# A second sort in fewer steps, a bias kept in a freed matrix row, and the combining of moe_1 spread over three attentions

## The reference, cut to what matters

```python
    logits = xt @ Wr + br;  p = softmax(logits);  probs, idx = top_k(p, 2)
    probs = probs / probs.sum(axis=-1, keepdims=True)
    h = jnp.einsum('td,edf->etf', xt, W1) + b1[:, None, :]
    h = _layernorm(jax.nn.relu(h), g1, be1)
    y = jnp.einsum('etf,efd->etd', h, W2) + b2[:, None, :]
    y = _layernorm(jax.nn.relu(y), g2, be2)
    out = jnp.einsum('te,etd->td', gate, y)      # gate: probs at the two chosen experts
```

## Time and profile before

| | |
|---|---|
| PE busy | 1710.9 us (90%) |
| PE weight loads | 1127.0 us (59%) |
| DVE busy | 1166.0 us (61%) |
| ACT busy | 778.5 us (41%) |
| POOL busy | 761.2 us (40%) |
| mean granted clock of the PE | 0.936 |
| transfers | 90.40 MB in 62796 packets |

### The profile page before, as it was taken

One profiled execution on the slowest core, in us unless ns is written; L12 is line 12 of the kernel. 1 busy time (PEld: TensorE's weight loads), 2 busy tenths in 40 slices (PEclk: granted clock), 3 DMA queues, 4 the chain that ended last, 5 costly groups with the idle time before them and its releaser, 6 DMA issues. The chain is left out here.

```text
span 1907.3 us, 30893 instructions
## 1 busy us (share of the span) xinstructions
PE 1710.9 (90%) x10309; PEld 1127.0 (59%) x10309; DVE 1166.0 (61%) x3041; ACT 778.5 (41%) x1965; POOL 761.2 (40%) x983
## 2 busy tenths in 40 slices
PE   5796698768899999999999997879999999999999
PEld 4544476535575657756577564546756565656656
DVE  6836666546756657657576564557757555554654
ACT  2411254315443646537466273126627422232222
POOL 3433545618746636656266462007647200000000
PEclk7865899889999999999999997989999999999999
DMA  8010022100000000000000000000000473643452
GB/s 299 1 28 13 27 81 70 40 17 15 9 1 1 2 1 1 1 1 2 1 2 1 1 2 1 1 1 1 1 1 2 133 204 120 201 120 113 130 168 84
DMA packets 62796, 90.40 MB, mean 47 GB/s; under 512 B 11056, under 2 KB 29104, under 8 KB 61872
## 3 DMA queue, kind: packets, MB, share of 16 engines
q1 hardware_dynamic: 60592, 84.23, 14.4%
q0 software_dynamic: 2048, 4.20, 0.8%
HBM read 78.43 MB, written 9.96 MB: 46 GB/s over the span
## 5 line engine op out<-in xcount | busy, mean ns | idle before, releaser
L1583 POOL TENSOR_TENSOR rows<-rows,rinv 128x512 f32<-128x512 f32 x192 | 197.1, 1054 | 139.6 <-DVE rinv L1821 139.6
L2492 ACT ACTIVATE region_b<-psum 128x512 f32<-128x512 f32 x132 | 78.8, 597 | 259.1 <-PE psum L2454 259.0
L1747 ACT ACTIVATE rows<-psum,nmax 128x512 f32<-128x512 f32 x192 | 130.2, 684 | 125.0 <-DVE nmax L1814 124.9
L2466 PEld LDWEIGHTS psum<-region_c,region_b 128*128 128x128 f32 x1024 | 132.1, 192 | 56.1 <-issue 43.4
L2530 DVE TENSOR_TENSOR region_b<-region_b,psum 128x512 f32<-128x512 f32 x128 | 87.9, 686 | 124.7 <-ACT region_b L2492 122.3
L1813 DVE TENSOR_REDUCE lg<-psum 128x2 f32<-128x1024 f32 x128 | 155.7, 1216 | 6.0 <-PE psum L1631 2.9
L1930 POOL TENSOR_TENSOR rows<-rows,rinv 128x128 f32<-128x128 f32 (+2 forms) x192 | 127.1, 683 | 77.4 <-DVE rinv L2099 77.4
L1825 DVE COPY turned<-psum 128x512 f32<-128x512 f32 x128 | 88.3, 690 | 92.3 <-PE psum L1643 92.0
L1631 PE MATMUL psum<-region_a,region_b 64*128 64x256 f32 x1024 | 134.0, 399 | 8.0 <-ACT rows L1747 5.6
L2094 DVE TENSOR_REDUCE nmax<-psum 128x1 f32<-128x128 f32 (+3 forms) x256 | 113.7, 486 | 42.4 <-PE psum L1976 41.4
L2466 PE MATMUL psum<-region_c,region_b 128*128 128x128 f32 x1024 | 133.5, 275 | 1.3 <-DVE region_b L2538 1.3
(11 more groups left out here) (752 smaller groups left out, 3600.4 us busy)
## 6 DMA issues: line engine op xcount, KB each, us to landing
pt<-gates SPq DMA_DIRECT2D x128, 128.0 KB, 3.0
ysb<-gates SPq DMA_DIRECT2D x128, 128.0 KB, 3.6
region_a<-in_eg SPq DMA_DIRECT2D x32, 256.0 KB, 3.4
region_a<-in_eu SPq DMA_DIRECT2D x32, 256.0 KB, 3.5
region_c<-in_weights SPq DMA_DIRECT2D x32, 256.0 KB, 4.7
sorted<-kctx SPq DMA_DIRECT2D x2, 1536.0 KB, 14.5
region_b<-sorted SPq DMA_DIRECT2D x12, 256.0 KB, 3.2
made<-rows SPq DMA_DIRECT2D x12, 256.0 KB, 2.4
```

Source lines behind the costliest of these rows:

```text
L1583: nc.gpsimd.tensor_tensor(row(u, j), row(u, j), rinv[:, 2 * u + j:2 * u + j + 1].broadcast_to([P, S]), ALU.mult).then_inc(s.pn, 1)
L1747: nc.scalar.activation(row(u, j), s_bank(u, j), ACT.Exp, bias=nmax[:, 2 * u + j:2 * u + j + 1], accum_out=sum_column(u // T, u % T, j)).th ...
L2466: mm = nc.tensor.matmul(bank(7)[:, P * t:P * (t + 1)], htb[:, i % 2, P * t:P * (t + 1)], wd, start=(i == 0 and t == 0), stop=(i == n_items ...
```

## The change

1. `fold_b1` is removed. In block 1, `w1` is loaded without its last row (127 of 128); for each expert one more transfer writes that last row to 127 partitions of a scratch tile (`last_row(e)`), and a single one puts the bias `b1` in the freed row 127. POOL subtracts the last row from the 127 others, one expert per step 20 to 27 of `setup`. The wait for w1 at the block's end is gone. The page's turned tokens keep 127 features, and partition 127 stays at 1.0, from a memset in `route_1`; the copy of a page is an ACT Copy over 127 partitions.
2. The scatters of `route_1` have their own steps: `step(10 + m / per_step)`, two per step in block 2, three in block 3. In block 3 the steps of routing are mapped as `(0, 0, 1, 2, 3, 4, 5, 6, 7, 8)` and those from 10 on to n - 2: 16 scatters after pages 8 to 13, where they were after pages 10 to 17.
3. In `pages_1` there are four hidden buffers instead of three; the relu of a quad's output is on DVE, behind the bias, and both stand in the quad's fourth page, where centring comes at the second and adding at the third; POOL makes hrs before rstd.
4. The last quad's relu, statistics, centring and adding leave block 3 (`last_rows_1`): DVE takes one piece ahead of each of the first projection copies of the first attention_2, POOL the rstd, SP the store, and ScalarE waits for the stored rows ahead of the first exponential.
5. `combine_1`: block 3 combines only batch 0 (a gather per page from page 33 on, the add after page 42, `norm_ahead` at 43/46). Batches 1, 2 and 3 are combined in the attention_2 of batches 0, 1 and 2, one gather at the head of steps 1 to 8, and one operation of the add at the end of steps 10, 11 and 12.

The core of the diff:

```diff
@@ load_first_matrices
             for e in range(E8):
-                sp.dma_start(w1[:, e, 0:F1], a["w1"][:, e, :]).then_inc(s.w1_in, 16)
+                sp.dma_start(w1[0:D - 1, e, 0:F1], a["w1"][0:D - 1, e, :]).then_inc(s.w1_in, 16)
+                sp.dma_start(last_row(e)[0:D - 1, :], a["w1"][D - 1:D, e, :].broadcast_to([D - 1, F1])).then_inc(s.w1_in, 16)
+            sp.dma_start(w1[D - 1:D, :, 0:F1], a["early"][0:E8, lo:lo + F1].rearrange("(o e) f -> o e f", o=1)).then_inc(s.w1_in, 16)
@@ setup, gpsimd
+                for e in range(E8):
+                    yield 20 + e
+                    if e == 0:
+                        pool.wait_ge(s.w1_in, 16 * (2 * E8 + 1))
+                    rows = w1[0:D - 1, e, 0:F1]
+                    nc.gpsimd.tensor_tensor(rows, rows, last_row(e)[0:D - 1, :], ALU.subtract)
@@ route_1, vector and gpsimd
+                    nc.vector.memset(page_t[96:P, :, :], 1.0)
-                for j in range(GT):
-                    yield step(10 + j)
-                    pool.wait_ge(s.r_slots, 1)
-                    for n in range(K1):
+                for m in range(K1 * GT):
+                    j, n = m // K1, m % K1
+                    yield step(10 + m / per_step)
+                    if m == 0:
+                        pool.wait_ge(s.r_slots, 1)
@@ pages_1, vector
-                if k % 4 == 2 and 0 <= q < n_quads:
-                    rows_bias(q)
-                if k % 4 == 3 and 0 <= q - 1 < n_quads:
-                    rows_centre(q - 1)
-                    rows_add(q - 1)
+                if k % 4 == 1:
...
+                    if 0 <= q - 1 < n_quads - 1:
+                        rows_centre(q - 1)
+                if k % 4 == 2 and 0 <= q - 1 < n_quads - 1:
+                    rows_add(q - 1)
+                if k % 4 == 3 and 0 <= q < n_quads:
+                    rows_bias(q)
+                    if q < n_quads - 1:
+                        rows_relu(q)
@@ last_rows_1 (new), vector
+                nc.vector.tensor_scalar(rows, rows, 0.0, None, ALU.max).then_inc(s.l_relu, 1)
+                yield
+                dve.wait_ge(s.l_relu, 1)
...
+                yield
...
+                yield
+                dve.wait_ge(s.l_rstd, 2)
...
@@ attention_2, gpsimd and vector
-                        if late and 1 <= n <= 8:
-                            late[(n - 1) // 4].gather(pool, 2 * ((n - 1) % 4), 2)
+                        if combined and 1 <= n <= K1 * T:
+                            combined.gather(pool, n - 1)
-                        for i, batch in enumerate(late):
-                            if n == 4 * i + 6:
-                                batch.add(dve)
+                        if n > K1 * T + 1:
+                            next(added, None)
@@ moe_1_pages
-            block_of(k, sync, main, [route_1(sr, 1, bank(7), lambda n: n),
-                                     combine_beside(combine_1(s1, 0, found_b[0]), 35, 37),
-                                     norm_ahead(s1, xs[0], ahead_w, bank(7), keys_of(0), 39, 42, LN_EPS),
-                                     combine_beside(combine_1(s1, 1, found_b[1]), 40, 44)])
+            route_at = (0, 0, 1, 2, 3, 4, 5, 6, 7, 8)
+            block_of(k, sync, main, [route_1(sr, 1, bank(7), lambda n: route_at[n] if n < 10 else n - 2, 3),
+                                     combine_beside(s1, 0, 33, 42),
+                                     norm_ahead(s1, xs[0], ahead_w, bank(7), keys_of(0), 43, 46, LN_EPS)])
```

More of the change, by code:

```diff
@@ L1207, in sync @@
             def sync(sp):
-                for q in range(n_quads + 5):
+                for q in range(n_quads + 4):
                     if 3 <= q < n_quads:
@@ new lines, in gpsimd, with combine_1, gather @@
+            def gpsimd(pool):
+                pool.wait_ge(s.l_mv, 4)
+                link = chained(pool, s.l_rstd)
+                link(nc.gpsimd.tensor_scalar(w.rstd2[:, :], w.mv[:, :, 1], LN_EPS, None, ALU.add))
+                nc.gpsimd.tensor_tensor(w.rstd[:, :], w.rstd2[:, :], neg_half[:, :], ALU.pow).then_inc(s.l_rstd, 1)
+            return record(sync=sync, wait_stored=wait_stored, vector=vector, gpsimd=gpsimd)
+        def combine_1(s, b):
+            g, i = b // 2, b % 2
+            found, found_at = found_1[b], found_b[b]
+            def gather(pool, m):
+                n, t = m // T, m % T
+                col = GT * n + T * i + t
+                nc.gpsimd.indirect_dma_start(found_at[:, n, t, :], None, made_1[g][:, :],
+                                             bass.IndirectOffsetOnAxis(ap=slots[:, g, col:col + 1], axis=0)).then_inc(found, 16)
@@ L1466, in combine_beside @@
-        def combine_beside(c, gather_at, add_at):
+            return record(gather=gather, add=add)
+        def combine_beside(s, b, gather_at, add_at):
+            c = combine_1(s, b)
             def tensor(pe):
@@ L1475, in vector @@
                 yield add_at
-                c.add(dve)
+                yield from (add_at for _ in c.add(dve))
             def gpsimd(pool):
                 yield gather_at
-                c.gather(pool)
+                for stored_third in (s.out_0, s.out_1, s.out_2):
+                    pool.wait_ge(stored_third, 16 * (QUADS // 3))
+                for m in range(K1 * T):
+                    yield gather_at + m
+                    c.gather(pool, m)
             return record(tensor=tensor, vector=vector, scalar=scalar, gpsimd=gpsimd)
@@ L1492, in keys_of, with attention_2 @@
             return copy
-        def attention_2(k, b, late=()):
+        def attention_2(k, b, combined=None, last=None):
             s = sems(k % 2, ATTENTION_2)
@@ L1573, in _ @@
                     clear_set(sp, 1 - k % 2)
+                    if last:
+                        last.sync(sp)
                 @block.gpsimd
@@ L1766, in _ @@
                     copy_ctx(0, bank(4))
-                    for batch in late:
-                        batch.wait_stored(act)
+                    if last:
+                        last.wait_stored(act)
                     exps(0)
@@ L1793, in _ @@
                 def _(dve):
+                    rows = last.vector(dve) if last else iter(())
                     for c in range(PAIRS):
+                        next(rows, None)
                         dve.wait_ge(s.pq, 2 * c + 2)
@@ L1833, in _ @@
                     ctx_max(0)
+                    added = combined.add(dve) if combined else iter(())
                     for n in range(steps + 1):
```

151 lines of the change are left out of this document (68 added, 83 removed).

## The result

The change makes the kernel slower: 1986.1 us (1982.25 to 1987.29, 4 runs) against 1905.35 (1902.86 to 1909.26, 4 runs), a ratio of 1.042 with a 95% interval of 1.039 to 1.044. I had forecast 1860. The profiled execution of the changed kernel took 1982.25 us, with a span of 1980.5, which is 73.2 more than the span before.

A forecast was written before the change was run, and what follows sets the result against it. Idle PE time in blocks 1 to 3 and the first attention_2 was taken as reachable, block 2 also at a low clock. +1.0 - 10 - 27.6 - 7 + 0.3 = -43.3 took the median 1903.54 to 1860 us, range 1846 to 1880.

The forecast's parts named there:

- Block 1: Bias folded in on POOL: seventeen w1 transfers land near 50, one subtraction stays uncovered, +1.0 us (0 to +3).
- My sign of being wrong: Wrong if block 1 waits for w1_in past 80, block 3 has a DVE wait over 8 us, or a batch's attention_2 grows over 8.
- Rival D: Block 1: one-row broadcast loads run one after the other at 11.9 us, ending at 123; kernel 1909 us; chance 0.04.
- Block 2: Without fold_b1's matmuls the links at L1103 and L920 start earlier and the block ends 10 us earlier (6 to 12).
- Block 3: Sort and hidden buffers 5.4, combining 17 and tail 5.2 together give -27.6 us (-18 to -31).
- the sort: Block 3: earlier scatters let quad 6's load land before PE wants it; 9.4 us lost becomes about 4, gain 5.4.
- The hidden buffer: Block 3: the fourth buffer takes most of DVE's add and normalising for batch 0, leaving PE about 2.4 us of waiting.
- one gather a page: Block 3: batch 0's gathers fit one per page from page 33, removing DVE's wait that cost PE 7.0 us.
- Attention_2: Batches 0 to 2: spread gathers (3.2 us a batch) and adds (1.5) cost 14.1 against 20.9, so -7 us (-14 to -2).
- Rival B: Attention_2: gathers and adds cost by the piece, +10.5 us instead of -7; kernel 1878 us; chance 0.11.
- The last quad's rows: First attention_2: 3.9 us of DVE work beside projection copies and 1.35 of POOL cost +0.3 us (0 to +0.5).
- The port rule: Block 3: relus moved to DVE block POOL's scatters and gathers, eleven times 0.5, about 6 us; kernel about 1866; chance 0.03.

The follow-up runs named there:

- even: The changed kernel with all w1 transfers over 128 rows and the bias sent to row 127 after they landed: 1866.07 us against 1908.7, 0.978.
- the repetition of `even`: The kernel of `even` unchanged, run once more on one chip beside other kernels: 1865.95 us against 1906.17 for the kernel before, 0.979.

## Why the prediction was wrong

**Block 1, the step that failed.** "2.1 MB more at the 375 to 410 GB/s of the full slices is 5 to 6 us, so the last lands near 50." The sum charged bytes at the rate of other transfers. They ran at 25 GB/s, the last landed at 198.7, and the step cost 123.4 instead of 1.0. The count of rows stood in the diff and I never asked what it does to the split over engines; none of the rows that I showed has a transfer over 127 partitions, so its price had no upper end, and I took it from the fastest rows. My sign of being wrong (a wait for w1_in past 80) came true. Rival D had the mechanism's place and its threshold right (late landing, beyond 119), but the wrong reason (one source row), a price of 11.9 for only eight of the seventeen, and a chance of 0.04. With sixteen at 10.57, one behind the other from 29.4, when their first packets run, it gives 198.5; 198.7 was measured. The +1.0 without this is 1.6 to 4.1 in runs with even transfers, because the subtractions hold DVE; they also take 1.23 each, with POOL alone too (7.36 for six, above), and not 1.04.

**Block 2: -10 forecast, -6.8 measured.** The links came where I put them: L1115 (L1103 before) starts 27.0 after the block's start, where the forecast had 26.0, and the first L931 (L920 before) at 36.1 against 33.8. The mistake was to take the first batch's ctx scores for the end of the gain; the second batch's came only 6.8 earlier than before, behind the routing's logits, and the block ends with them.

**Block 3: -27.6 forecast, -30.7 measured.** A fair total, in part from wrong causes, and so in part luck. By the starts of the quads, quad 7 begins 5.3 earlier than before (68.7 instead of 74.0 after the block's start), just the 5.4 that I gave the sort; by the last quad it is 8.0, and the other 22.7 come behind that. But a DVE wait over 8 us, another of my signs of being wrong, does stand in block 3 (the 10.63 shown above), and from quad 5 to quad 6 go 15.0 us where an undisturbed quad takes 9.2, so 5.8 are lost and not 4. The relu on DVE, costed at nothing, carries 8.1. The scatters' steps are worth 3.0. The hidden buffer, to which I gave the room for DVE, is worth 0.1, and one gather a page instead of eight in a row 2.3, where I had put it at most of 7. The remaining 17 or so (one batch combined less, hrs before rstd, the last quad's tail) were not taken apart.

**Attention_2: -7 forecast for the three, -15.2 measured** (129.3 to 110.3, and 108.3 to 110.2 twice, by L1595). Both terms were too dear. A batch's gathers, put at 3.2, cost 2.0: step 0 to 1 takes 13.3 instead of 12.0 and the next two together 13.8 instead of 12.0, but steps 3 to 9 take 41.0 instead of 42.2, because steps of 6.3 and 7.7 us became steps of about 7. The spread add, put at 1.5, costs nothing: steps 9 to 15 take 42.1, without an add 42.2. Rival B ("by the piece") falls. The whole of the second and third attention_2 grew by 0.3 and 3.6 instead of 1.9 each; that comes from the clock: the first 23 us of the second before, and of the third after, were granted 0.93, the other way round 1.00.

```profile
666.80:690.00 23.20, 22.71 (x78) 12.24 (x79) 8.69 (x14) 5.73 (x10) 0.92 (x1) 0.93 0.00 1
```

```profile
731.90:754.00 22.10, 21.63 (x80) 11.51 (x78) 9.56 (x16) 6.65 (x14) 0.64 (x2) 1.00 0.00 1
977.10:1000.00 22.90, 22.43 (x78) 11.89 (x78) 8.70 (x14) 5.74 (x10) 0.56 (x1) 0.93 0.00 1
```

**The last quad's rows: +0.3 forecast.** The first L1595 stands 24.6 after the start, 25.2 before: nothing to see.

**The port rule** of the Trainium skill (SBUF — State Buffer, "Who interferes with whom") was weighed at the wrong place. Of the eleven relus on DVE in the changed kernel eight take 0.43, and the three slower ones, 0.48 to 0.58, run beside an indirect transfer; the scatters beside relus take 0.96 as before, and only one gather, in `even`, took 1.20 instead of 0.95. It struck in block 1 in the other direction: POOL held the shared ports first, and each of DVE's four operations took as long as the subtraction beside it (1.24 instead of 0.28). That is what the rule says of the one that comes second, and it was to be had from the page together with L619 of the kernel before, which is that operation and runs its four from 71.0 on, where I put the subtractions.

## What to carry to other kernels

Count the rows of every transfer that a change touches, before its bytes: 127 rows instead of 128 made a 256 KB load take 10.5 us instead of about 0.7 (the eight of the kernel before land 0.7 to 1.6 us apart), and a row can be written by a small transfer of its own afterwards. A transfer whose shape no row of the trace has should get the slowest near rate as its upper end, and what waits for it in an engine's queue ahead of unrelated work should be listed with it. Spread small POOL and DVE pieces one per step and move them where the other of the two engines is idle.

## What the runs showed of the hardware

- A load or broadcast over 127 partitions moved at 25 GB/s, one engine's share (6.5% of 16), 83 ns per 2 KB row; over 128, an issue stands 0.4 to 2.9 us. 126, 120, 112, 104, 96 and 64 rows showed at most 0.8 us; 124 rows showed 2.3 us and 4.2 engines busy.
- A broadcast of one 2 KB row of device memory to 128 partitions was as fast as a load of 128 different rows.
- POOL's 127x512 subtraction with both inputs in on-chip memory stretched a DVE tensor_scalar of 128x128 beside it from 0.28 to 1.24 us.
- Left open: in block 3's scatters, five profiled executions of `even`'s and its variants' code (of eleven with this order of work) had a block 3 that was 6.7 to 7.9 us longer (9.9 and 10.2 with the gathers packed), in which ScalarE stood up to 8.8 us, PE 6.8 and DVE 7.7. For two of the five the profile puts ScalarE's wait down to issue, for three to a weight load issued some 40 us earlier. All five are on two chips, where each run of this order showed it, and `even`'s own code showed it on one chip and not on another. What holds ScalarE there wasn't found. ScalarE's row in the repetition of `even`:

```profile
268.67 0.60 ACT L1304 ACTIVATE turned<-psum 128x512 f32<-128x512 f32 x1 [0.88 <-PE psum L1267]
278.06 0.60 ACT L1311 ACTIVATE turned<-psum 128x512 f32<-128x512 f32 x1 [8.79 <-issue]
```
